# Second cross attention and gated expert layer of a two-layer decoder as one phase, with routing and row scatters following the attention group by group

## The reference, cut to what matters

```python
x = x + L0_attn(layernorm(x)); x = x + L0_xattn(layernorm(x), ctx); x = x + L0_ffn(layernorm(x))
x = x + L1_attn(layernorm(x))
x = x + L1_xattn(layernorm(x), ctx, ctx)      # 16 heads of 8, 64 keys in each sequence
x = x + L1_ffn(layernorm(x))

def L1_ffn(x):                                # 8 experts, the best 2 for each token
    probs = softmax(x @ router_w.T)
    mask = one_hot_of_top2(probs)
    probs = probs * mask / (sum(probs * mask) + 1e-9)
    h = silu(x @ gate_w + gate_b) * (x @ up_w + up_b)
    return einsum('ne,ned->nd', probs, h @ down_w + down_b)
```

## Time and profile before

| | us |
|---|---|
| median of 3 runs | 1899.2 |
| the three runs | 1881.14, 1905.21, 1899.2 |
| the profiled execution | 1887.83 |
| its span (first to last instruction) | 1886.0 |

### The profile page before, as it was taken

The page is one execution under the profiler, slowest core; times in us unless marked ns, Lnnn a source line. Parts: engine busy times, 40 slices in busy tenths (PEclk is TensorE's granted clock), DMA queues, the critical chain, the costliest instruction groups (busy, mean ns, idle before and its releaser), DMA issues. The chain is left out here.

```text
span 1886.0 us, 27391 instructions
## 1 busy us (share of the span) xinstructions
PE 1285.3 (68%) x9658; PEld 838.4 (44%) x9658; DVE 1112.4 (59%) x2432; ACT 773.6 (41%) x1360; POOL 842.1 (45%) x618
## 2 busy tenths in 40 slices
PE   5678777777767368883214996399859996224992
PEld 2233233233223146563214996166636665224882
DVE  2899989989997357653431111577625763442335
ACT  3544545544532155551002553276625772002331
POOL 2666666666673267771662554110010110564552
PEclk8798898898998578875556998599956996556996
DMA  4102102102100510003115775500030001115675
GB/s 157 69 23 96 68 28 96 69 28 96 69 28 6 121 18 2 2 2 96 38 43 170 228 226 163 130 7 19 13 98 1 19 13 50 50 42 172 212 214 165
DMA packets 106652, 148.38 MB, mean 79 GB/s; under 512 B 14029, under 2 KB 82938, under 8 KB 102228
## 3 DMA queue, kind: packets, MB, share of 16 engines
q1 hardware_dynamic: 95220, 128.94, 22.7%
q0 software_dynamic: 9088, 17.07, 2.6%
q10 hardware_dynamic: 2208, 0.61, 0.1%
HBM read 113.96 MB, written 34.45 MB: 79 GB/s over the span
## 5 line engine op out<-in xcount | busy, mean ns | idle before, releaser
L889 POOL TENSOR_TENSOR M_dbx<-M_u,M_b_sb 128x1024 f32<-128x1024 f32 x128 | 300.0, 2355 | 128.9 <-DVE M_h L976 127.6
L976 DVE TENSOR_TENSOR_SCAN M_h<-M_pA,M_dbx 128x512 f32<-128x512 f32 x256 | 310.8, 1214 | 6.0 <-POOL M_dbx L889 5.0
L1127 ACT ACTIVATE M_pA<-M_dt,M_a_neg 128x504 f32<-128x504 f32 x256 | 173.8, 683 | 277.4 <-DVE M_h L976 276.5
L1244 PE MATMUL M_pY<-M_hc,M_ident 128*128 128x512 f32 x512 | 279.4, 675 | 6.3 <-DVE M_y_sum L994 6.3
L1499 POOL DMA_INDIRECT F_answers<-F_yblk,F_xblk x156 | 151.5, 971 | 159.5 <-DVE F_yblk L1627 118.0
L986 DVE TENSOR_TENSOR M_hc<-M_h,M_pC 128x512 f32<-128x512 f32 x256 | 169.4, 662 | 35.9 <-issue 23.3
L1492 POOL DMA_INDIRECT F_slots<-F_line,F_pos x128 | 125.4, 979 | 68.3 <-issue 48.0
L1755 PE MATMUL F_bank<-F_xT,F_wbuf 128*128 128x256 f32 x624 | 153.9, 391 | 0.9 <-ACT F_xT L1670 0.9
L1244 PEld LDWEIGHTS M_pY<-M_hc,M_ident 128*128 128x128 f32 x512 | 108.9, 214 | 94.1 <-issue 81.2
L1232 PE MATMUL M_pC<-M_split,M_sel_bf 96*128 96x512 bf16 x128 | 53.9, 421 | 133.2 <-DVE M_hc L986 132.9
L357 DVE TENSOR_REDUCE X_smax<-X_pS 128x8 f32<-128x512 f32 x128 | 82.4, 685 | 99.6 <-PE X_pS L598 99.6
(11 more groups left out here) (260 smaller groups left out, 2304.6 us busy)
## 6 DMA issues: line engine op xcount, KB each, us to landing
M_b_sb<-M_rows_bc SPq DMA_DIRECT2D x32, 1024.0 KB
F_wbuf<-in_F_wcat SPq DMA_DIRECT2D x39, 578.0 KB
F_wbuf<-in_F_wcat SPq DMA_DIRECT2D x39, 450.0 KB
F_xblk<-F_slots SPq DMA_DIRECT2D x78, 132.0 KB
F_ya<-F_answers SPq DMA_DIRECT2D x16, 512.0 KB, 7.0
x<-X_x SPq DMA_DIRECT2D x16, 256.0 KB
X_kv<-in_ctxT SPq DMA_DIRECT2D x2, 1344.0 KB, 10.1
F_answers<-F_yblk,F_xblk POOLq DMA_INDIRECT x156
```

Of the source, the lines that this page charges most:

```text
L889: pool.tensor_tensor(dbx[:, k % DBXS, :, :], u[:, g % 2, :, :], bc(b_sb[:, n, :], 1, 2), ALU.mult).then_inc(dbx_ready, 1)
L976: v.tensor_tensor_scan(h[:, k % STATES, half, :], pA[:, (2 * k + half) % DECAYS, :, :].rearrange("p b t -> p (b t)"), dbx[:, k % DBXS, hal ...
L1127: act.activation(pA[:, (2 * k + half) % DECAYS, :, 1:SEQ], dt[:, g % 2, half, :].rearrange("p (b t) -> p b t", t=SEQ)[:, :, 1:SEQ], ACT.Ex ...
L1244: ins = pe.matmul(pY[:, half, :], ident[:, :], hc[:, k % HCS, half, :], start=(n == 0), stop=(n == N - 1))
```

## The change

`cross_expert_phase` takes the place of the two calls. Three functions hold the parts: `attention_stage` (the attention's operations), `dispatch_stage` (LayerNorm, router, choice, ranks and scatters) and `expert_stage` (the blocks and the sum, same operations as before). x is loaded once and stays in SBUF. A loop of 46 steps runs the 32 attention steps, and beside them, for group c-2: residual and statistics on DVE in step 0 of group c, application of the LayerNorm on POOL and the transpose on PE in step 1, router and choice in step 3; for group c-3 ranks and place in step 1; and from step 14 on two indirect DMAs in each step, so that the rows of group 7 leave in steps 42 to 45. The application of the attention's own LayerNorm moves from DVE to POOL. `project_o` moves from step 0 of the next group to the end of step 3, behind `turn_o` of the same group. The second copy of the normalised rows, which ACT made (L1657), becomes a DMA from SBUF to SBUF issued by SP. Constants of the dispatch are loaded behind all of x. Weights of block 0 are asked for before the wait for the rows. The buffers of the answers lie in `kT` and in the softmax's work buffers.

```diff
--- before.py
+++ after.py
...
+def attention_stage(nc, m, pre, w, x, bank, ident, ctxT=None, streamed=False):
...
+    def pool_start(pool):
+        pool.memset(ln.minus_half[:, :], -0.5).then_inc(consts, 1)
+        pool.memset(everything(vd), 0.0).then_inc(consts, 1)
+        for hl in range(2):
+            pool.wait_ge(consts, 2 + hl)
+            pool.memset(vd[hl * HALF:(hl + 1) * HALF, :, :, :, hl, HD:COLS], 1.0).then_inc(consts, 1)
+        pool.wait_ge(consts, 4)
+        rstd(pool, 0)
+        if streamed:
+            normal(pool, 0)
+        rstd(pool, 1)
+        if streamed:
+            normal(pool, 1)
+        pool.wait_ge(bias_ready, 1)
...
+    def tensor_step(pe, i, own=None, before=None, q_after=None, o_after=None):
+        c, s = i // PER, i % PER
+        soon = c + 1 < GROUPS
+        if i < STEPS:
+            scores(pe, i)
+        if own is not None:
+            own(pe, i)
+        if before is not None:
+            before(pe, i)
+        if 2 <= i < STEPS + 2:
+            weights_times_v(pe, 2 * i - 4)
+            weights_times_v(pe, 2 * i - 3)
+        if 1 <= i <= STEPS:
+            turn_weights(pe, 2 * i - 2)
+        if soon:
+            if s == 0:
+                turn_x(pe, c + 1)
+            if s == 1:
+                project_k(pe, c + 1)
+            if s == 2:
+                if q_after is not None:
+                    q_after(pe, c + 1)
+                project_q(pe, c + 1)
+        if s == 3 and in_range(c - 1):
+            turn_o(pe, c - 1, o_after)
+        if 1 <= i <= STEPS:
+            turn_weights(pe, 2 * i - 1)
+        if s == 2 and soon:
+            project_v(pe, c + 1)
+        if s == 3 and in_range(c - 1):
+            project_o(pe, c - 1)
...
+def dispatch_stage(nc, m, pre, w, att, x, bank, ident, gated):
...
+    def sync_rows(sp):
+        for g in range(GROUPS):
+            sp.wait_ge(xn_ready, g + 1)
+            reach(sp, scattered[g % RING], 16 * 2 * TILES * (g // RING))
+            sp.dma_start(line[:, g % RING, 1, :, 0:D], line[:, g % RING, 0, :, 0:D]).then_inc(twin_in[g % RING], 16)
+        sp.wait_ge(tail_ready, 1)
+        for e in range(E):
+            t = sp.value_load(tail[0:1, e:e + 1], min_val=0, max_val=E * CAP - BLOCK)
+            sp.dma_start(slots[bass.ds(t, BLOCK), :].rearrange("(p s) c -> p s c", s=SUBS),
+                         pad[:, :, :]).then_inc(pads_in, 16)
...
+    def pool_start(pool):
+        pool.memset(ln.minus_half[:, :], -0.5).then_inc(consts, 1)
+        pool.memset(pad[:, :, 0:D], 0.0).then_inc(consts, 1)
+        pool.memset(pad[:, :, D:ROW].bitcast(I32), 2 * TOKENS).then_inc(consts, 1)
+        pool.memset(ones_bf[:, :], 1.0).then_inc(consts, 1)
+        pool.memset(line[:, :, :, :, D:ROW], 0.0).then_inc(consts, 1)
+        pool.memset(carry[:, 0, :], 0.0).then_inc(consts, 1)
+        pool.wait_ge(consts, 6)
+        pool.wait_ge(consts_in, 16 * NW)
...
+    def pool_normal(pool, g):
+        pool.wait_ge(var_ready, g + 1)
+        pool.tensor_tensor(ln.rstd[:, :], ln.var_eps[:, :], ln.minus_half[:, :], ALU.pow).then_inc(rstd_ready, 1)
+        pool.wait_ge(rstd_ready, g + 1)
+        reach(pool, scattered[g % RING], 16 * 2 * TILES * (g // RING))
+        pool.tensor_copy(line[:, g % RING, :, :, D:D + 1].bitcast(I32).rearrange("p k t o -> p k (t o)"),
+                         ids[:, g, :, :]).then_inc(id_ready, 1)
+        for t in range(TILES):
+            ins = pool.tensor_scalar(line[:, g % RING, 0, t, 0:D], xg(g)[:, t, :], ln.mean[:, t:t + 1],
+                                     ln.rstd[:, t:t + 1], ALU.subtract, ALU.mult)
+        ins.then_inc(xn_ready, 1)
...
+    def stats(v, link, g):
+        v.wait_ge(att.y_done, g + 1)
+        reach(v, xn_ready, g)
+        layer_norm_stats(v, link, xg(g), ln)
+        v.tensor_tensor(ln.var_eps[:, :], ln.m2[:, :], ln.dm2[:, :], ALU.add).then_inc(var_ready, 1)
...
+    def scalar_turned(act, i):
+        c, s = i // PER, i % PER
+        if s == 1 and in_range(c - 2):
+            g = c - 2
+            act.wait_ge(xT_psum, g + 1)
+            reach(act, lg_psum, g)
+            act.activation(xnT[:, :], pM[:, 0, :], ACT.Identity).then_inc(xnT_ready, 1)
...
+    def turn_x(pe, g):
+        pe.wait_ge(xn_ready, g + 1)
+        pe.wait_ge(att.xnT_ready, min(g + 4, GROUPS))
+        reach(pe, att.ot_ready, min(g + 1, GROUPS))
+        for t in range(TILES):
+            ins = pe.transpose(pM[:, 0, t * P:(t + 1) * P], line[:, g % RING, 0, t, 0:D], ident[:, :])
+        ins.then_inc(xT_psum, 1)
...
+    def own(pe, i):
+        j = i - 1 if i % 2 == 0 else i - 2
+        c, s = j // PER, j % PER
+        reach(pe, att.o_used, normalised(j))
+        reach(pe, lg_read, at_most(0, c - 1 if s == 3 else c - 2, GROUPS))
+        reach(pe, rank_read, at_most(0, c - 2, GROUPS))
...
+    def tensor_before(pe, i):
+        c, s = i // PER, i % PER
+        if s == 3 and in_range(c - 2):
+            logits(pe, c - 2)
+        if s == 1 and in_range(c - 3):
+            ranks(pe, c - 3)
+            if c - 3 == GROUPS - 1:
+                counts(pe)
...
+def cross_expert_phase(nc, apre, fpre, w, src, dst, ctxT):
+    LAST = STEPS + 14
...
+        @block.sync
+        def _(sp):
+            def load(part):
+                g, n = parts[part]
+                sp.dma_start(x[:, g * TILES:(g + n) * TILES, :],
+                             src.rearrange("(n p) d -> p n d", p=P)[:, g * TILES:(g + n) * TILES, :]
+                             ).then_inc(x_in[part], 16)
+            load(0)
+            a.sync_loads(sp)
+            load(1)
+            load(2)
+            d.sync_loads(sp)
+            d.sync_rows(sp)
+            f.sync_blocks(sp)
...
+        @block.gpsimd
+        def _(pool):
+            d.pool_start(pool)
+            a.pool_start(pool)
+            for i in range(LAST):
+                c, s = i // PER, i % PER
+                if s == 0 and c < GROUPS:
+                    a.pool_add_bias(pool, c)
+                if s == 1:
+                    if in_range(c - 2):
+                        d.pool_normal(pool, c - 2)
+                    if c + 2 < GROUPS:
+                        a.pool_rstd(pool, c + 2)
+                if s == 2 and c + 2 < GROUPS:
+                    a.normal(pool, c + 2)
+                g, n = (i - 14) // PER, (i - 14) % PER
+                if i >= 14 and in_range(g):
+                    d.pool_scatter(pool, g, n)
+            f.pool_answers(pool)
+        @block.vector
+        def _(v):
+            link = linker(v, Count(chain, 0))
+            def x_wait(v, g):
+                v.wait_ge(x_in[g], 16)
+            a.vector_start(v, link, x_wait)
+            d.vector_start(v)
+            v.wait_ge(x_in[2], 16)
+            for i in range(LAST):
+                c, s = i // PER, i % PER
+                a.vector_softmax(v, i)
+                if s == 0 and in_range(c - 2):
+                    a.residual(v, c - 2)
+                    d.stats(v, link, c - 2)
+                if s == 3 and in_range(c - 2):
+                    d.choose(v, link, c - 2)
+                if s == 1:
+                    if in_range(c - 3):
+                        d.place(v, link, c - 3)
+                    if c + 2 < GROUPS:
+                        a.layer_norm(v, link, c + 2)
+            d.vector_table(v, link)
+            f.vector_blocks(v)
+            v.wait_ge(d.weight_ready, 1)
+            for g in range(GROUPS):
+                f.vector_sum(v, link, g, d.weight)
+        @block.scalar
+        def _(act):
+            a.scalar_start(act)
+            a.scalar_first(act)
+            for i in range(LAST):
+                a.scalar_step(act, i, d.scalar_turned)
+            d.scalar_exp(act)
+            f.scalar_blocks(act)
+        @block.tensor
+        def _(pe):
+            a.tensor_start(pe)
+            d.tensor_start(pe)
+            for i in range(LAST):
+                a.tensor_step(pe, i, d.own, d.tensor_before, d.q_after, d.o_after)
+                if i % PER == 1 and in_range(i // PER - 2):
+                    d.turn_x(pe, i // PER - 2)
+            f.tensor_blocks(pe)
...
-    attention_phase(nc, "X1", w, between[3], between[4], w["ctxT"])
-    sparse_ffn_phase(nc, "F1", w, between[4], y, gated=True)
+    cross_expert_phase(nc, "X1", "F1", w, between[3], y, w["ctxT"])
```

702 lines of the change are left out of this document (added).

## The result

| | median us | runs |
|---|---|---|
| before | 1890.11 | 20 |
| after | 1912.38 | 20 |

The ratio is 1.0101, 95% interval 1.0072 to 1.0131: the change makes the kernel 1% longer. (The 1899.2 us from which the forecast of 1863 was worked out is the median of three runs; that of twenty is 1890.11.) The profiled execution of after has a span of 1910.9 us, against 1886.0.

The account below looks back on a forecast made before the run. TensorE paces the attention; then 64 indirect DMAs (82 us) fill most of 128 us before block 0. Start +14, groups of 26.5 and drain 55 put block 0 34.8 us earlier; weights about 1: gain 36, 1899.2 to 1863, range 1826 to 1896.

Parts of the forecast that it names:

- The start, +14: Phase start: POOL waits for dispatch constants behind x, so first scores come 14 us later; bounds 0 (or gain) and 17.
- The work added: Loop, TensorE: 17.6 us busy a group, plus 1.8 us for router, transposes and ranks.
- The order, as waits: Loop, TensorE's in-order queue: waits for LayerNorm, split copy_k and copy_oT make a group 23.8 us, before clock and signals.
- The clock, +1.7 a group: Loop: looser TensorE work lowers the clock to about 0.85, as in the first cross attention; 1.7 us a group.
- Signals held back, +1.0 a group: Loop: TensorE's finished instructions are seen late beside POOL's indirect DMAs; 1.0 us a group, bounds 0 and 2.4.
- The second rival: Loop: TensorE's signals are held back as in the dispatch, 9.2 us more a group, +51, 1914 us; chance 0.12.
- The drain, 77 us from step 28: Loop's end to block 0: group 7 takes 22 us, then 55 us follow, 8 of these for late signals.
- The rest, 0: Block 0 to the end (blocks, answers, sum): the same 168 us as before, no change.
- The first rival: Loop stays tight: TensorE's new 1.8 us and little else, 22.0 us a group, 1835 us; chance 0.20.
- The third: Loop: POOL becomes the bound as scatters stretch to 2.56 us beside VectorE's work, +18, 1881 us; chance 0.10.

Follow-up runs that it names:

- e1_start: Changed kernel, POOL's wait for the dispatch constants moved to its first dispatch LayerNorm, constants requested before x's last part, taken up later by VectorE and TensorE; ratio to before 0.9923.
- e2_order: Changed kernel with ScalarE's and TensorE's attention order put back to the kernel before's (whole copy_k, copy_v, project_o one step later); ratio to before 0.9929.
- e6_combo: Changed kernel with constants off the start, the attention order of the kernel before, and both LayerNorm applications on VectorE; ratio to before 0.9888.
- e11_late_third: Changed kernel with an eight-group row buffer and all 64 scatters issued after the loop, third run of this kernel; five groups took 146.5 us.
- r1_before: Kernel before, unchanged, profiled again beside later runs; 1863 us, loop groups of 19.24 us.
- r2_after: Changed kernel, unchanged, run again beside later runs; ratio to before 1.0156, groups of 29.8 to 38.9 us.
- r3_after: Changed kernel, unchanged, as the reference on the chip of e11_late_third; five groups took 161.2 us.
- e8_turn_vector: Changed kernel with the edits of e1_start and e2_order, dispatch transposes moved into mid step 2, both LayerNorm applications on VectorE; 1794 us beside 1834.7 of before.
- e12_turn_vector: Kernel of e8_turn_vector run again, on a chip where the kernel before took 1889.78 us; median 1858.54 us, ratio to before 0.9817.

## Why the prediction was wrong

The forecast was 1863 us; 1912.38 is above its range. Its picture of the gain was right, its prices of the loop were not.

- **The start, +14: direction right, 8 us short.** The mechanism is shown (e1_start, 20 us back). The constants came at 1413.70 and not at 1406.5, because SP's first issue of them took 10.55 us; POOL's LayerNorm was 3.15 us and not 2.0. These two are the 8 us. (The terms listed for the start add to 1414.0 and not 1414.3, and the 0.9 us from the end of the bias product to the scores have no row.) The bound of 17 let the constants be 3 us later; they were 7.
- **The work added: right.** 19.34 us of TensorE a group at full clock, against 19.4 counted.
- **The order, as waits: right places, wrong order of size.** `project_o` behind `copy_oT` and the split `copy_k` are where TensorE waits (1.1 to 1.6 and 1.1 us, forecast 1.5 and 0.3), and step 1 where it waits for LayerNorm (forecast 1.0; 2.9 and 2.7 in e2_order and e6_combo, nearly nothing in after, where the other waits make the room).
- **The clock, +1.7 a group: this is the term that failed.** I took 0.86 from the first cross attention and added 1.7 us. In after it is 0.60 to 0.74. In e1_start a group without late signals has TensorE busy 25.7 to 26.5 us for the work of 19.3, some 7 us more, and lasts 28.5 to 29.6 us; with 23.8 for steps and waits as forecast, that leaves 5 to 6 us a group and not 1.7. Five groups without scatters on kind A (e11_late_third) took 146.5 us, where the forecast without its 1.0 for signals has 25 + 4 x 25.5 = 127: 20 us missed here. On kind B e2_order shows that the attention's order makes 11 us of it (145.7 to 135.0; 15 with the first eight steps). The place of the dispatch's transposes makes 14 us in these five groups (135.0 to 120.9) and nothing over the whole loop. Why the same amount of waiting goes with a clock of 0.73 in one order and 0.82 in another is open.
- **Signals held back, +1.0 a group: the second that failed.** They cost 15 to 20 us of the loop on this kind of chip, 4 to 5 us a group where scatters run. The second rival had the mechanism (9.2 a group and 1914 in all). That its time nearly came out is luck: there are two causes of about equal weight, of which it had only one, and it priced that one at 51 us more where some 16 were measured. I gave it 0.12 because pairs of DMAs lose little in the blocks; in the loop POOL is behind its own work and issues four to six in a row.
- **The drain, 77 us from step 28: 12 short on kind A, right on kind B by luck** (77.5 in e1_start, where none of the 8 us for held signals is needed). SP's padding took 20.3 us and not the 15.6 of the earlier trace rows, and from the counts to block 0 it was 24.1 for the 19.0 used; on kind B it is 16.2. The 8 us for held signals were too few.
- **The rest, 0: +7.7.** From the first to the last yblk it is 128.8 in after and 129.0 in r1_before, so 6 us of it are the spread of the kernel before, whose first profile had 122.6. From block 0 to the end r1_before has 172.7, r2_after and r3_after 176.8 and 175.6: 3 to 4 us remain, for whose cause no run was made.
- **The first rival** (loop tight, 22.0) is what the loop would be at full clock: one group of e8_turn_vector has 22.1. **The third** did not come. In e12_turn_vector, where VectorE applies LayerNorm beside the scatters, these are 1.27 us apart (its timeline):

```profile
1580.65 1.34 DVE L123 TENSOR_SCALAR X_xn<-X_x,X_ln_mean,X_ln_rstd 128x128 f32<-128x128 f32 x4
...
1580.97 0.97 POOL L2347 DMA_INDIRECT F_slots<-F_line,F_pos  x1 [0.30 <-issue]
1582.24 0.97 POOL L2347 DMA_INDIRECT F_slots<-F_line,F_pos  x1 [0.30 <-issue]
```

The Trainium skill (SBUF — State Buffer, Who interferes with whom) says that the building of GpSimd's descriptors starves while VectorE holds the port that the two share; these rows, as the earlier trace rows, don't show it. It is VectorE whose four instructions took longer here, 1.34 us for the 1.11 of the earlier trace rows.

The sum in short: forecast gain 36, missed 8 (start), 32 (loop; 20 by order and clock and 16 by signals, taken from e11 and after, less 4 in the first eight steps, which took 48.0 us for the 51.5 forecast), 12 (drain), 8 (rest) = 60, a loss of 24 against the profiled execution of before, which is what the two profiles show (1910.9 and 1886.0).

## What to carry to other kernels

Price a wait that is added to TensorE's queue in a loop at full clock at twice its length and more: its own time and the half-clock stretches behind it (a group of e2_order, with one wait of 2.9 us, is 4.9 us longer than the group of e8_turn_vector that kept full clock). Don't count on getting all of that back: with this wait gone the five groups were 2.8 us shorter each and the whole loop no shorter. Measure the whole loop, its first steps too. A stage that merely overlaps two others gains what the shorter one leaves only if the pacing engine's order stays free of new waits; look at the order before the sums of busy time. And put constants that a later part needs behind nothing that an earlier part waits for: let each engine wait for them at first use.
